# The last two chunks of the final output tile made group by group, the fifth group in two column halves

## The reference

```python
q = _split_heads(hidden_states @ Wq.T, H)
k = _split_heads(text @ Wk.T, H)
v = _split_heads(text @ Wv.T, H)
out_text = _merge_heads(_attend(q, k, v, sm_scale))
...
out = out_text + IP_SCALE * out_ip
out = out @ Wo.T + bo
return out + residual
```

## Time and profile before

| what | value |
|---|---|
| median of 3 runs | 426.36 us (426.17 to 426.8) |
| profiled execution's own time | 425.95 us |
| its span in the trace | 424.2 us |
| PE, DVE, ACT, POOL busy | 98%, 62%, 71%, 72% |
| granted TensorE clock, mean | 1.0 of full speed |

### The profile page before, as it was taken

How to read it: one execution, slowest core, us unless ns; L and a number is a source line. 1 busy time by engine, 2 the same in 40 slices (tenths; PEclk the granted TensorE clock), 3 DMA queues, 4 the chain that set the end, 5 groups by cost and what they waited for, 6 DMA issues and landing times.

```text
span 424.2 us, 8270 instructions
## 1 busy us (share of the span) xinstructions
PE 416.4 (98%) x2550; PEld 237.9 (56%) x2550; DVE 263.1 (62%) x544; ACT 301.1 (71%) x585; POOL 306.0 (72%) x267
## 2 busy tenths in 40 slices
PE   8999999999999999999999999999999999999996
PEld 6977765677777755544444444444444444444442
DVE  0354676755676687776577656765677655556723
ACT  1737888847477788989767975888667966966720
POOL 8327799999659599798959594769649594764560
PEclk9999999999999999999999999999999999999999
DMA  8997636444844576454753347334743446345203
GB/s 276 372 331 264 222 115 221 153 155 147 280 156 157 186 249 218 158 163 144 257 191 125 131 151 245 126 134 174 251 166 129 147 134 239 133 168 192 83 25 125
DMA packets 41781, 77.33 MB, mean 182 GB/s; under 512 B 5264, under 2 KB 6416, under 8 KB 41744
## 3 DMA queue, kind: packets, MB, share of 16 engines
q1 hardware_dynamic: 30944, 57.21, 38.9%
q10 hardware_dynamic: 10800, 19.67, 14.3%
HBM read 33.40 MB, written 10.49 MB: 103 GB/s over the span
## 4 chain that ended last, share of the span: by engine, by line
PE 93%; ACT 2%; issue 1%; DVE 1%; POOL 1%; DMA 1%; DVEq 0%; POOLq 0%; ACTq 0%
PE ps_q L932 30%; PE ps_o L932 27%; PE ps_s L999 10%; PE ps_pv L1006 7%; PE ps_m L983 5%; PE ps_den L1011 4%; PE ps_o L904 2%; PE ps_m L1056 1%; PE ps_s L891 1%; DMA q_packed<-mxT 1%; PE ps_q L883 1%; PE ps_q L1056 1%; PE ps_s L1056 1%; PE ps_o L1056 1%; PE ps_den L891 1%
## 5 line engine op out<-in xcount | busy, mean ns | idle before, releaser
L451 POOL TENSOR_TENSOR p_lo<-p_f,p_hi 77x512 f16<-77x512 f32 x160 | 183.0, 1165 | 85.2 <-ACT p_hi L586 84.2
L582 ACT ACTIVATE p_f<-ps_s 77x512 f32<-77x512 f32 x160 | 94.3, 589 | 22.1 <-PE ps_s L999 20.9
L720 DVE TENSOR_REDUCE mx<-ps_m 128x4 fp32r<-128x308 f32 x160 | 69.2, 475 | 44.6 <-PE ps_m L983 43.7
L586 ACT ACTIVATE p_hi<-ps_s 77x512 f16<-77x512 f32 x160 | 93.5, 584 | 2.4 <-PE ps_den L1011 2.4
L932 PE MATMUL ps_o<-attn,wo 128*128 128x512 f16 x360 | 90.2, 381 | 0.4 <-DVE sums L795 0.2
L932 PE MATMUL ps_q<-x,wq 128*128 128x512 f16 x375 | 85.1, 379 | 0.0
L999 PE MATMUL ps_s<-q_packed,k_packed 128*77 128x512 f32 x160 | 63.4, 439 | 0.2
L932 PEld LDWEIGHTS ps_q<-x,wq 128*128 128x128 f16 x375 | 36.5, 98 | 44.3 <-issue 0.8
L932 PEld LDWEIGHTS ps_o<-attn,wo 128*128 128x128 f16 x360 | 29.5, 98 | 38.9 <-issue 10.9
L709 DVE SCALAR_TENSOR_TENSOR q_lo<-ps_q,q_scale,q_hi 128x512 fp32r<-128x512 f32 x25 | 18.8, 751 | 48.6 <-ACT q_hi L565 48.6
L983 PE MATMUL ps_m<-k_diag,q_hi 128*128 128x308 f32 x160 | 42.2, 343 | 0.5 <-ACT q_hi L565 0.5
(11 more groups left out here) (127 smaller groups left out, 660.5 us busy)
## 6 DMA issues: line engine op xcount, KB each, us to landing
q_packed<-q_hi SPq DMA_DIRECT2D x80, 256.0 KB, 2.5
x_f<-in_x SPq DMA_DIRECT2D x45, 256.0 KB, 4.0
q_packed<-q_lo SPq DMA_DIRECT2D x40, 256.0 KB, 3.2
x_res<-in_x ACTq DMA_DIRECT2D x35, 256.0 KB, 2.7
out<-x_res ACTq DMA_DIRECT2D x35, 256.0 KB, 2.7
wq_sb<-in_wq SPq DMA_DIRECT2D x10, 320.0 KB, 4.5
wo_sb<-in_wo SPq DMA_DIRECT2D x10, 320.0 KB, 4.0
wk_sb<-in_wk SPq DMA_DIRECT2D x8, 320.0 KB, 5.4
```

The lines of the kernel that those rows point to most:

```text
L451: nc.gpsimd.tensor_tensor(p_lo[:, i, :], p_f[:, i, :], p_hi[:, i, :], ALU.subtract).then_inc(plo_done, 1)
L582: nc.scalar.activation(p_f[:, i, :], ps_s[i % 2][0:L, :], ACT.Exp, scale=SCALE).then_inc(pf_done, 1)
L586: nc.scalar.activation(p_hi[:, i, :], ps_s[i % 2][0:L, :], ACT.Exp, scale=SCALE).then_inc(phi_done, 1)
L720: nc.vector.tensor_reduce(mx[:, g % RS, :, tt], ps_m[tt % 2][:, 0:HG * L].rearrange("p (h k) -> p h k", k=L), AX_X, ALU.max).then_inc(max_ ...
```

## The change

Chunks 1 and 2 of the last tile are still made chunk by chunk over all groups. Chunks 3 and 4 are now made together, group outermost: group 0's six matmuls, then group 1's, and so on. The fifth group (k = 4), in every chunk, is split into two halves of 256 columns, each with a bank of its own (`ps_s0` and `ps_s1`); each half has its own three matmuls per chunk, its own `finish_out`, its own count and its own store of 128 KB, 1 KB for each partition.

```diff
+        def last_parts(k):
+
+            if k < G - 1:
+                return [(ps_last[k], slice(0, TB))]
+            return [(ps_s[0], slice(0, TB // 2)), (ps_s[1], slice(TB // 2, TB))]
...
             def store(t, k):
+                if is_last(t):
+                    for n, (_, cols) in enumerate(last_parts(k)):
+                        act.wait_ge(outs_done, nth(t, k) + n + 1)
+                        act.dma_start(out[t, k, :, cols], x_f[:, k, cols]).then_inc(last_in, 16)
+                    return
                 act.wait_ge(outs_done, nth(t, k) + 1)
-                if is_last(t):
-                    act.dma_start(out[t, k], x_f[:, k, :]).then_inc(last_in, 16)
-                    return
...
-            act.wait_ge(last_in, 16 * G)
+            act.wait_ge(last_in, 16 * (G + 1))
...
                 if is_last(t):
-                    dve.wait_ge(last_done, k + 1)
                     dve.wait_ge(last_biased, k + 1)
-                    nc.vector.scalar_tensor_tensor(x_f[:, k, :], out_bank(t, k)[:, :], out_scale[:, k:k + 1],
-                                                   x_f[:, k, :], ALU.mult, ALU.add).then_inc(outs_done, 1)
+                    for n, (ps, cols) in enumerate(last_parts(k)):
+                        dve.wait_ge(last_done, k + n + 1)
+                        nc.vector.scalar_tensor_tensor(x_f[:, k, cols], ps[:, cols], out_scale[:, k:k + 1],
+                                                       x_f[:, k, cols], ALU.mult, ALU.add).then_inc(outs_done, 1)
                     return
...
-            def last_tiles(c):
+            def last_tiles(chunks):
 
                 w_hi, w_lo, a_hi, a_lo = halves(wo_16, attn_16)
-                wait_attn(NB - 1, c)
-                for k in range(G):
+                for c in chunks:
+                    wait_attn(NB - 1, c)
+                for k, c in itertools.product(range(G), chunks):
...
-                    for n, (w, a) in enumerate(((w_hi, a_hi), (w_lo, a_hi), (w_hi, a_lo))):
-                        last = nc.tensor.matmul(ps_last[k][:, :], w[:, k, P * c:P * (c + 1)], a[:, c, :],
-                                                start=(c == 0 and n == 0), stop=(c == G - 1 and n == 2))
-                    if c == G - 1:
-                        last.then_inc(last_done, 1)
+                    for ps, cols in last_parts(k):
+                        for n, (w, a) in enumerate(((w_hi, a_hi), (w_lo, a_hi), (w_hi, a_lo))):
+                            last = nc.tensor.matmul(ps[:, cols], w[:, k, P * c:P * (c + 1)], a[:, c, cols],
+                                                    start=(c == 0 and n == 0), stop=(c == G - 1 and n == 2))
+                        if c == G - 1:
+                            last.then_inc(last_done, 1)
...
-                    last_tiles(0)
+                    last_tiles((0,))
                 if isinstance(t, int) and t == NB:
-                    for c in range(1, G):
-                        last_tiles(c)
+                    for chunks in ((1,), (2,), (3, 4)):
+                        last_tiles(chunks)
```

More of the change, by code:

```diff
@@ L1 @@
 import numpy as np
+import itertools
 from contextlib import ExitStack
```

## The result

The changed kernel takes 425.86 us (median of 22 runs, 425.48 to 426.98) beside 426.51 for the kernel before in the same sets of runs. The ratio of the two is given as 0.9987, with a 95% interval from 0.9981 to 0.9993: 0.55 us faster, 0.3 to 0.8 (the two medians taken alone are 0.65 apart). The change is less than the 0.2% that the prediction took as the least that can be told from none, but the interval doesn't contain 1, so it is a change. The time is 0.11 above the forecast 425.75.

What follows compares the result with a forecast made beforehand. PE's stream was taken as the bound, with only the stretch behind its end movable. Earlier issue 0.22, less waiting 0.13 and shorter transfer 0.27 make 0.62 us; 426.36 - 0.6 = 425.75, range 425.2 to 426.65.

Steps and rivals of the forecast that it cites:

- What bounds the kernel: Whole span: PE is busy 98%, its columns stay, so only the stretch behind its last matmul can move.
- Interleaving costs nothing: Start of chunks 3 and 4: POOL has chunk 4's low half 1.9 us early, so PE doesn't wait; price nothing.
- Half matmuls at 0.110: Fifth group on PE: weight loads stay hidden, 0.110 us per 256-column matmul, 0.04 us more in all.
- Halves on DVE: Fifth group's last operations: 0.471 us per half, the second starting 0.385 behind the first and ending at 421.26.
- The issue of the last store: ACT's queue at the end: free at 421.30, just as the second half is ready, for 421.52 before; 0.22 us gained.
- The size of a small transfer: Fifth group's stores on the DMA engines: 0.42 us per half, between bounds 0.34 and 0.69; shorter transfer gains 0.27.
- The sum: Kernel's end: last packet at 422.60 for 423.22, 0.62 us earlier, made of 0.22, 0.13 and 0.27.
- the wait behind the fourth store: Last store on the DMA engines: its waiting for the store ahead falls from 0.16 to 0.03 us, 0.13 gained.
- B: Last stores: small packets cost as much as large ones, 0.69 us per half; gain 0.08, time 426.28; chance 0.17.
- C: Fifth group on DVE: each half pays a full operation; gain 0.1, time 426.25; chance 0.03.
- D: All 30 half matmuls: weight loads aren't hidden, 0.205 us each, stream 2.9 us longer, time 428.65; chance 0.08.
- E: Last store: second half also lands faster and its packets halve to 0.34; gain 0.9, time 425.45; chance 0.15.

Runs made afterwards that it cites:

- pieces of 128: Changed kernel with groups 0 to 3's matmuls in chunks 3 and 4 cut into 128-column pieces, each with its own weight load: 20.87 us from mark to span's end.
- order only: Changed kernel with the fifth group whole, one bank and one 256 KB store, chunks 3 and 4 still group by group: ratio 1.0000 to the kernel before.
- halves only: Changed kernel with all four chunks chunk by chunk over the groups, the fifth group still in two halves: ratio 1.0001 to the kernel before.

## Why the prediction was right

*What bounds the kernel.* That PE's stream stays and only what lies behind it moves was right: from the mark to the start of chunk 3 it is 11.01 us before and 11.03 after, and the whole gain is behind PE's end.

*Interleaving costs nothing.* Right. There is no idle time of PE at 414.74. POOL had the low half at 411.63 + 1.16 = 412.79, 1.95 us early (predicted 1.9).

*Half matmuls at 0.110.* Right: 0.109, the 15 additional ones cost 0.03 us in all (17.68 for 17.65), and the pieces of 128 show that there was room for twice the division.

*Halves on DVE.* 0.471 predicted from the 256-column row, 0.475 and 0.484 measured; the second started 0.40 behind the first instead of 0.385. What was too small is the handover from PE: 0.04 from the record's end to DVE's start in the earlier trace rows, but 0.10 here (the first half's last matmul record ends at 421.07, DVE starts at 421.17), and 0.11 for group 0 and for the fifth group of order only. The order alone therefore brought no earlier issue. It isn't the order that lengthens the handover, for halves only has it too, chunk by chunk (group 0's last record ends at 418.67, DVE starts at 418.77). All changed versions share one more edit of `finish_out`, which the prediction doesn't price: the wait on `last_biased` now stands ahead of the one on `last_done`. Whether that is the cause stays open; no run turns the two back. Together this made the last issue 0.15 earlier, not 0.22.

*The issue of the last store.* The prediction took from the earlier trace rows that ACT's queue is free again 0.39 later, and that was exact (421.69 and 422.08). It overlooked the second figure of those rows: the issue directly behind another takes 0.45 instead of 0.35. In the changed kernel it delays the packets by 0.1, and it opened the dip at 423.0. With SP issuing the last store, the dip and 0.10 us went away.

*The size of a small transfer.* 0.42 predicted by a line between 512 B and 2 KB, 0.39 measured. The 91 ns of the packets of 1,232 B don't carry over to these stores; whether they came from the start of the kernel or from reading is not shown. The Trainium skill, "DMA: Bandwidth & Descriptors", section "Why a DMA increments its semaphore by 16 and not by 1", has 2 KiB per partition as the least that saturates the engines on earlier generations. This case agrees in direction only: 1 KB rows move 128 KB in 0.39 us, 336 GB/s, and 2 KB rows 256 KB in 0.69, 380 GB/s, so small rows are 12% slower, and far from costing as much as whole ones.

*The sum.* The last packet came 0.45 earlier, not 0.62, and the span's end with it. The shortfall of 0.17 is the issue (0.07) and the delay of the last store's packets (0.10). The other two terms were right: with the last store on SP's queue, from its issue to its last packet it is 1.39 us, where order only has 1.67 for a whole store, so the shorter transfer gives 0.28 (predicted 0.27); and order only has 1.67 where the kernel before has 1.78, so the wait behind the fourth store gives 0.11 (predicted 0.13). The tail behind the last packet was taken as unchanged, and it is; its size was read as 1.0 and is 0.85, since windows of 0.1 us put the last packet too early, at 423.22 instead of 423.30, which moves nothing in the difference. The runs' 0.55 lies closer to the forecast 0.6 than the trace's 0.45 does, but the interval of the runs, 0.3 to 0.8, is too wide for that to say anything. The mechanism was right; two terms, the handover and the price of a second issue, were missing or too small.

*The rivals.* B is refuted by the 0.39 us of a half. C by the 0.48 us of DVE's halves. D by the 0.109 and 0.056 between matmuls. E didn't occur: a half store lands 1.8 us after its issue instead of 2.0, but with the tail at 0.85 in both kernels that is the shorter transfer and nothing besides, and the gain stayed under 0.85 us.

## What to carry to other kernels

The end of a kernel is a short pipeline of its own: last matmul, DVE's operation that takes the result out of its bank, issue, transfer, completion. Making the last piece smaller pays only if the stages behind it are idle when it comes; here the halves alone lost 0.18 us, the order alone gained 0.09, and both together 0.45. Add up such a tail stage by stage and ask for each what it is still busy with, queues included; the next bound (here the transfers, 0.15 us further) shows up in the same table.

Effects of half a microsecond are read in the trace from a mark near the change, not from the span: twelve executions of ten kernels with the same instructions up to the mark reached it anywhere from 403.00 to 403.82 us. And the end has to be read as finely as the mark: with spans rounded to 0.1 us the order alone would seem to gain 424.2 - 403.00 less 424.1 - 403.09, which is 0.19 instead of 0.09.

## What was not expected of the hardware

A weight load whose record lasts 98 ns was hidden behind matmuls only 56 ns apart. A DMA issue directly behind another on ACT's queue took 0.43 to 0.47 us instead of 0.34, and where the DMA engines were free (the changed kernel) its packets began 0.1 us later as well. A store of 128 KB in 1 KB rows took 56% of the engine time of one of 256 KB in 2 KB rows. From the last packet to the end of the kernel it took 0.84 to 0.86 us in all twelve executions, whichever queue had issued the last store and whatever its size.
